# Sums of an attention sorted by DMA instead of transposed on TensorE

## The reference

```python
v = values.reshape(N, -1, HEADS, HEAD) @ Wv.T
k = keys.reshape(N, Lk, HEADS, HEAD) @ Wk.T
q = queries.reshape(N, Lq, HEADS, HEAD) @ Wq.T
energy = jnp.einsum('bqhd,bkhd->bhqk', q, k)
energy = jnp.where(mask, energy, jnp.float32(-1e+20))
attn = jax.nn.softmax(energy / np.sqrt(HEAD), axis=-1)
out = jnp.einsum('bhqk,bkhd->bqhd', attn, v).reshape(N, Lq, EMBED)
return out @ Wo.T + bo
...
x = x + jnp.tanh(g_xattn[1]) * _L1_xattn_ref(ctx_1024, ctx_1024, _layernorm(x, axis=-1), mask_1x1xSxS2_bk0, ...)
```

## Time and profile before

| | |
|---|---|
| median of 3 runs | 1335.78 us (1335.64 to 1337.21) |
| the profiled execution's own time | 1333.82 us |
| its span in the trace | 1332.1 us |
| second attention, first scores to last values product | about 231 to 382 us of the span |
| its projection and additions | about 386 to 413 us |
| busy in the whole span: PE, DVE, ACT, POOL | 1208.9, 1001.2, 835.0, 227.6 us |
| mean granted TensorE clock | 0.968 |

### The profile page before, as it was taken

How to read it: one execution, slowest core, us unless ns; L and a number is a source line. 1 busy time by engine, 2 the same in 40 slices (tenths; PEclk the granted TensorE clock), 3 DMA queues, 4 the chain that set the end, 5 groups by cost and what they waited for, 6 DMA issues and landing times.

```text
span 1332.1 us, 26357 instructions
## 1 busy us (share of the span) xinstructions
PE 1208.9 (91%) x10562; PEld 559.8 (42%) x10562; DVE 1001.2 (75%) x1491; ACT 835.0 (63%) x1484; POOL 227.6 (17%) x176
## 2 busy tenths in 40 slices
PE   4888964999999999778999999999999999999988
PEld 2566753555566456243333232323233333332237
DVE  4895695665536768458999999999999999999702
ACT  1224673777743642115888878787787878887861
POOL 2130124554742423800000000000000000000000
PEclk8979996999999999888999999999999999999999
DMA  6100027566500334812424533244423444243003
GB/s 189 26 1 15 1 31 166 96 110 129 96 1 1 119 119 144 124 24 49 64 51 76 86 60 65 53 87 80 57 59 67 87 64 67 50 82 50 2 1 126
DMA packets 78825, 92.55 MB, mean 69 GB/s; under 512 B 15210, under 2 KB 53356, under 8 KB 78704
## 3 DMA queue, kind: packets, MB, share of 16 engines
q1 hardware_dynamic: 78704, 90.87, 34.5%
HBM read 67.02 MB, written 23.80 MB: 68 GB/s over the span
## 4 chain that ended last, share of the span: by engine, by line
PE 60%; DVE 29%; ACT 5%; issue 2%; DMA 1%; SPq 1%; POOL 1%; DVEq 0%; ACTq 0%; POOLq 0%
DVE sm L2083 19%; PE ps L1554 10%; PE ps L1545 9%; PE ps L1526 6%; ACT W L1021 3%; PE ps L1415 3%; PE ps L1321 2%; PE ps L1664 2%; PE ps L1312 2%; PE ps L1313 2%; PE ps L1374 2%; PE ps L1481 1%; PE ps L1536 1%; PE ps L1279 1%; PE ps L1277 1%
## 5 line engine op out<-in xcount | busy, mean ns | idle before, releaser
L2083 DVE TENSOR_REDUCE sm<-ps 128x1 f32<-128x1024 f32 x512 | 599.7, 1218 | 31.4 <-PE ps L1526 28.1
L1021 ACT ACTIVATE W<-ps 128x512 f32<-128x512 f32 x1024 | 534.8, 605 | 139.2 <-PE ps L1554 135.2
L1554 PE MATMUL ps<-R 99*32 99x512 bf16 x4096 | 317.8, 383 | 6.2 <-ACT W L1021 3.2
L1545 PE MATMUL ps<-W,R 128*32 128x512 f32 x2048 | 265.6, 594 | 0.7 <-ACT W L1021 0.7
L1554 PEld LDWEIGHTS ps<-R 99*32 99x32 bf16 x4096 | 86.3, 94 | 224.4 <-ACT W L1021 168.0
L803 POOL COPY R<-R 128x512 f32<-128x512 f32 x16 | 9.8, 613 | 633.1 <-PE ps L1545 633.1
L1526 PE MATMUL ps<-R 50*128 50x512 bf16 x512 | 89.1, 388 | 15.8 <-DVE sm L2083 13.1
L1526 PE MATMUL ps<-KM,R 50*128 50x512 bf16 x512 | 87.3, 384 | 9.6 <-DVE sm L2083 6.6
L945 ACT ACTIVATE R<-ps 77x512 f32<-77x512 f32 x128 | 75.1, 592 | 23.6 <-PE ps L1313 14.2
L1545 PEld LDWEIGHTS ps<-W,R 128*32 128x32 f32 x2048 | 63.1, 111 | 42.1 <-ACT W L1021 1.4
L1866 DVE TENSOR_REDUCE small<-ps 128x4 bf16<-128x308 f32 x128 | 57.5, 473 | 23.5 <-PE ps L1279 23.4
(11 more groups left out here) (262 smaller groups left out, 1565.3 us busy)
## 6 DMA issues: line engine op xcount, KB each, us to landing
R<-x_parts SPq DMA_DIRECT2D x96, 128.0 KB, 4.9
R<-q_parts SPq DMA_DIRECT2D x192, 64.0 KB
R<-q_parts SPq DMA_DIRECT2D x96, 128.0 KB
R<-k_parts SPq DMA_DIRECT2D x96, 128.0 KB
x_parts<-R SPq DMA_DIRECT2D x8, 768.0 KB, 6.8
q_parts<-R SPq DMA_DIRECT2D x24, 256.0 KB, 2.6
k_parts<-R SPq DMA_DIRECT2D x24, 256.0 KB, 2.6
X<-in_x SPq DMA_DIRECT2D x4, 1024.0 KB, 9.8
```

The source lines that it names most:

```text
L1021: act.activation(PR[:, s % 2, h, :], third_bank("score", 64 * u + n), ACT.Exp, scale=0.25).then_inc(s_sfree, 1)
L1545: mm = pe.matmul(bank(7)[32 * h:32 * h + 32, :], VST[j][:, k, h, :], PR[:, s % 2, h, :], start=(k == 0), stop=(k == TB - 1))
L1554: mm = pe.matmul(o[32 * c:32 * c + 32, :], KST[j][0:MAX_ROW + 1, h, t:t + 32], QST[j][0:MAX_ROW + 1, h, 512 * (s // 8):512 * (s // 8) + 51 ...
L2083: dve.tensor_reduce(MX[:, half, h, q:q + 1], bank(2 * ((p + 1) % 2), 2), AX, ALU.max).then_inc(s_tfree, 1)
```

## The change

The sums stay with heads on partitions, as they come out of the values product. `out_transposes1`, `normalise1`, `transposes1` and ScalarE's copies of `OnT` go.

After `copy_out1(m)` SP issues eight DMAs, all inside SBUF (`sort_out1`): four take the denominator row of a head, 512 numbers in one partition, and spread it over 32 partitions of 16 numbers (`Rd1`, four half units deep), and four take the 16 rows of a head's sums to their place in `OT1`, which has the channels on the partitions and the tokens along the free axis, the form the projection reads. `copy_out1(m + 2)` waits for these DMAs of `m`, since it writes the same half of `Oe`.

VectorE inverts 128x16 denominators in place (`invert_sums1`, three half units behind). SP writes the inverses to DRAM (8 KB), waits until they have landed, and reads them back with each head's row given to 16 partitions (`spread_factors1`, three half units behind the sorting, 128 KB into `Den1`). Two units then lie on 128 partitions, and one multiplication of 128x512 divides both (`divide_pair1`). The projection of chunk `c` waits for the divisions of its batch alone; the last two divisions stand in VectorE's list behind the additions of the first batch and ahead of its statistics.

In SP's list the sorting and spreading of unit u - 3 stand behind `load_x_stack(u)` and the writes of parts. The semaphores of two bias steps are merged, which changes no wait.

```diff
+            def sort_out1(m):
+                u, q = m // 2, m % 2
+                b, rows, j = u // 4, 64 * (u % 2), u // 2 % 2
+                sp.wait_ge(s_oc, m + 1)
+                for h in range(4):
+                    sp.dma_start(Rd1[32 * h:32 * h + 32, m % 4, :],
+                                 Oe[32 * h + 16:32 * h + 17, q, :].rearrange("p (a n) -> p a n", a=32)
+                                 ).then_inc(s_od1[q], 16)
+                for h in range(4):
+                    v = slice(rows + 16 * h, rows + 16 * h + 16)
+                    sp.dma_start(OT1[v, j, b, 512 * q:512 * q + 512],
+                                 Oe[32 * h:32 * h + 16, q, :]).then_inc(s_od1[q], 16)
+
+            def spread_factors1(m):
+                u, q = m // 2, m % 2
+                pair, rows = u // 2, 64 * (u % 2)
+                sp.wait_ge(s_ri1, m + 1)
+                if u >= 1:
+                    sp.wait_ge(s_dd1[q], 32 * u)
+                sp.dma_start(DR1[m % 4].rearrange("(p n) -> p n", p=P), Rd1[:, m % 4, :]).then_inc(s_dd1[q], 16)
+                sp.wait_ge(s_dd1[q], 32 * u + 16)
+                if pair >= 2:
+                    sp.wait_ge(s_nd1, 2 * (pair - 2) + q + 1)
+                sp.dma_start(Den1[pair % 2][rows:rows + 64, q, :],
+                             DR1[m % 4].rearrange("(h n) -> h n", h=4).unsqueeze(1).to_broadcast([4, 16, 512])
+                             ).then_inc(s_dd1[q], 16)
+
+            def store_sums1(u):
+                for m in (2 * u, 2 * u + 1):
+                    sort_out1(m)
+                    if m >= 3:
+                        spread_factors1(m - 3)
...
             for u in range(UNITS):
...
                 load_x_stack(u)
                 for c in WRITES.get(u, ()):
                     write_parts(c)
+                if u >= 3:
+                    store_sums1(u - 3)
...
+            for u in range(UNITS - 3, UNITS):
+                store_sums1(u)
+            for m in range(2 * UNITS - 3, 2 * UNITS):
+                spread_factors1(m)
...
             def copy_out1(m):
                 act.wait_ge(s_pv, m + 1)
                 if m >= 2:
-                    act.wait_ge(s_ot1, m - 1)
+                    act.wait_ge(s_od1[m % 2], 128 * (m // 2))
                 act.copy(Oe[:, m % 2], bank(7)).then_inc(s_oc, 1)
...
-            for c in range(NC):
-                act.wait_ge(s_onT, c + 1)
-                if c >= 2:
-                    act.wait_ge(s_wo, c - 1)
-                act.copy(OnT[:, c % 2], bank(2 * (c % 2), 2).rearrange("p (j t) -> p j t", j=2)).then_inc(s_onc, 1)
...
-            def out_transposes1(m):
-                pe.wait_ge(s_oc, m + 1)
-                if m >= 1:
-                    pe.wait_ge(s_on, m)
-                for i in range(4):
-                    mm = pe.transpose(bank(3)[:, P * i:P * i + P], Oe[:, m % 2, P * i:P * i + P], identF[:, :])
-                mm.then_inc(s_ot1, 1)
...
-                if m >= 2:
-                    out_transposes1(m - 2)
...
-            pe.wait_ge(s_on, 2 * UNITS)
-            transposes1(0)
...
             for c in range(NC):
-                if c + 1 < NC:
-                    transposes1(c + 1)
-                pe.wait_ge(s_onc, c + 1)
+                b, q = c // 2, c % 2
+                pe.wait_ge(s_nd1, 4 * b + 3 + q)
                 if c == 1:
                     pe.wait_ge(s_qc, 3)
+                    pe.wait_ge(s_oc, 2 * UNITS)
...
-                        mm = pe.matmul(o, OnT[:, c % 2, j, P * i:P * i + P], wo1[:, j, :],
+                        mm = pe.matmul(o, OT1[:, j, b, 512 * q + P * i:512 * q + P * i + P], wo1[:, j, :],
...
-            def normalise1(m):
+            def invert_sums1(m):
+                dve.wait_ge(s_od1[m % 2], 128 * (m // 2 + 1))
+                if m >= 4:
+                    dve.wait_ge(s_dd1[m % 2], 32 * (m // 2 - 1))
+                dve.reciprocal(Rd1[:, m % 4, :], Rd1[:, m % 4, :]).then_inc(s_ri1, 1)
+
+            def divide_pair1(m):
                 u, q = m // 2, m % 2
-                b, hg = u // 4, u % 4
...
+                b, pair = u // 4, u // 2
+                dve.wait_ge(s_dd1[q], 32 * (u + 1))
+                o = OT1[:, pair % 2, b, 512 * q:512 * q + 512]
+                dve.tensor_tensor(o, o, Den1[pair % 2][:, q, :], ALU.mult).then_inc(s_nd1, 1)
...
-                if m >= 2:
-                    normalise1(m - 2)
+                if m >= 3:
+                    invert_sums1(m - 3)
+                if m >= 6 and (m - 6) // 2 % 2 == 1:
+                    divide_pair1(m - 6)
...
-            normalise1(2 * UNITS - 2)
-            normalise1(2 * UNITS - 1)
+            divide_pair1(2 * UNITS - 6)
+            invert_sums1(2 * UNITS - 3)
+            divide_pair1(2 * UNITS - 5)
+            invert_sums1(2 * UNITS - 2)
+            invert_sums1(2 * UNITS - 1)
...
             for b in range(B):
                 x3_batch(b)
+                if b == 0:
+                    divide_pair1(2 * UNITS - 2)
+                    divide_pair1(2 * UNITS - 1)
                 if b + 1 < B:
                     stats3(range(TB * b, TB * b + TB))
                     aggregate3(b)
```

More of the change, by code:

```diff
@@ L219, in build_program @@
               for v in (R4[0:SR1, 0:2048], R5[0:SR1, 0:2048], R5[0:SR1, 2048:4096])]
-        On = R1[:, :].rearrange("p (i c) -> p i c", i=NT)
-        OnT = R3f[:, 0:2048].rearrange("p (u j n) -> p u j n", u=2, j=2)
+        OT1 = R1[:, :].rearrange("p (j b t) -> p j b t", j=2, b=B)
+        Rd1 = R2f[:, 5946:6010].rearrange("p (u n) -> p u n", u=4)
+        Den1 = [v.rearrange("p (q n) -> p q n", q=2) for v in (R2f[:, 7168:8192], R3f[:, 7168:8192])]
         Mn = small[:, 464:496].bitcast(BF16).rearrange("p (u q j) -> p u q j", u=2, q=8)
-        rc1 = small[:, 528:544].rearrange("p (q j) -> p q j", q=4)
         s_w1 = sem("layer1_weights_loaded")
@@ L250, in build_program @@
         s_oc = sem("out1_copied")
[L251 to L255, removed]
+        s_od1 = [sem(f"out1_sorted{n}") for n in range(2)]
+        s_dd1 = [sem(f"out1_factors_moved{n}") for n in range(2)]
+        s_ri1 = sem("out1_recip")
+        s_nd1 = sem("out1_divided")
+        s_gb = sem("gated_biases")
+        s_xb = sem("biases_added")
         s_onT = sem("heads_transposed")
@@ L275, in score_bank1 @@
             return bank(4 + n % 3)
+        DR1 = nc.dram_tensor("sum_factors1", (4, 4 * 512), F32).ap()
         QP = nc.dram_tensor("q_parts", (3, B * C, S), BF16).ap()
@@ L351, in build_program @@
         s_c2 = sem("class_constants")
-        s_gb2 = sem("gated_bias2")
-        s_xb2 = sem("bias2_added")
         s_qp = sem("qkv_product")
@@ L781, in _ @@
             pool.tensor_tensor(qgn, qgn, mhalf[:, 0:2], ALU.pow).then_inc(s_qc, 1)
-            pool.tensor_scalar(bp2[:, :], bp2[:, :], gates[:, 3:4], None, ALU.mult).then_inc(s_gb2, 1)
+            pool.tensor_scalar(bp2[:, :], bp2[:, :], gates[:, 3:4], None, ALU.mult).then_inc(s_gb, 1)
             ln_rstd(3, range(B - 1))
@@ L812, in _ @@
                 pool.wait_ge(s_one, j + 1)
-            pool.wait_ge(s_gb2, 1)
+            pool.wait_ge(s_gb, 2)
             pool.wait_ge(s_xn, 4 * NC)
@@ L816, in _ @@
                 xs = X[:, TB * b:TB * b + TB, :]
-                pool.tensor_tensor(xs, xs, bp2[:, :].unsqueeze(1).to_broadcast([P, TB, C]), ALU.add).then_inc(s_xb2, 1)
+                pool.tensor_tensor(xs, xs, bp2[:, :].unsqueeze(1).to_broadcast([P, TB, C]), ALU.add).then_inc(s_xb, 1)
             for u in range(UNITS - 2):
@@ L1047, in _ @@
                 n = NC + c
-                act.wait_ge(s_onT, n + 1)
+                act.wait_ge(s_onT, c + 1)
                 if c >= 2:
@@ L1428, in _ @@
             transposes3(0)
-            pe.wait_ge(s_onc, NC)
             pe.wait_ge(s_wq3, 16)
@@ L1644, in transposes2 @@
                 if c >= 2:
-                    pe.wait_ge(s_onc, n - 1)
+                    pe.wait_ge(s_onc, c - 1)
                 for j in range(2):
@@ L1657, in _ @@
                     transposes2(c + 1)
-                pe.wait_ge(s_onc, n + 1)
+                pe.wait_ge(s_onc, c + 1)
                 if c >= 2:
@@ L1876, in maxima1 @@
                 reduce1(u, range(v.start + 2, v.stop))
-            def normalise1(m):
-                u, q = m // 2, m % 2
-                b, hg = u // 4, u % 4
[L1881 to L1889, removed]
+            def invert_sums1(m):
[4 more added lines that the diff above has]
+            def divide_pair1(m):
+                u, q = m // 2, m % 2
+                b, pair = u // 4, u // 2
+                dve.wait_ge(s_dd1[q], 32 * (u + 1))
+                o = OT1[:, pair % 2, b, 512 * q:512 * q + 512]
+                dve.tensor_tensor(o, o, Den1[pair % 2][:, q, :], ALU.mult).then_inc(s_nd1, 1)
             maxima1(0)
@@ L2139, in _ @@
                 dve.wait_ge(s_wo, NC + c + 1)
-                dve.wait_ge(s_xb2, c // 2 + 1)
+                dve.wait_ge(s_xb, B + c // 2 + 1)
```

## The result

The changed kernel takes 1495.55 us (median of 4 runs, 1490.64 to 1498.62) against 1335.71 us: a ratio of 1.119, 95% interval 1.1162 to 1.1218. It is slower by 160 us where 68 to 70 were forecast, and above the upper end of the range, 1470. The profiled execution took 1490.64 us with a span of 1488.9, 156.8 more than before.

What follows compares the result with a forecast made beforehand. SP's in-order issue queue was to bound the stage: loads 35.1, sorts 119.3, steps 66.1 and other issues 2.9 make 223.4 us; with the tail + 70.6 us on 1333.8, so 1404 us, range 1352 to 1470.

Steps and rivals of the forecast that it cites:

- What bounds the kernel after: Second attention: SP's in-order issue queue becomes the bound, 14.3 us a unit against TensorE's 8.2.
- the forecast names: Sign in the profile: ScalarE's copies, VectorE's reciprocals or TensorE's scores stand behind DMA.
- The price of a sorting issue: SP's queue, second attention: 0.466 us for each of 256 sorting DMAs, together 119.3 us.
- the dear end of my pitch: Upper bound for one sorting issue on SP, from a row spread into one partition: 0.608 us.
- the dear end of the whole sum: All SP prices at their upper bounds: 296 us of SP work, + 143 us, 1477 us.
- The wait after the write: SP waits 1.6 us for each write of inverses to land; with the read, 32 steps of 2.07 us.
- the fourth rival: Each unit's first inverses write lands late behind the six loads: 16 steps cost 3.3 us more, 1457 us; chance 0.07.
- The read back itself: SP's issue of each read back of the inverses, priced at 0.466 us.
- The tail: After SP's end at 461.3 us: last divisions, additions and projections end 21.3 us later, at 482.6; before, 411.99.
- the first rival: Second attention: sorts fit beside the rest, TensorE stays the bound, - 18.3 + 3.6 = - 14.7 us, 1319 us; chance 0.06.
- the third rival: Second attention: TensorE's clock falls to 0.50, its work 16.4 us a unit against SP's 14.3, 1451 us; chance 0.09.
- the mark of a TensorE near 60% busy: Sign that the forecast is right: TensorE near 60% busy in the second attention.

Runs made afterwards that it cites:

- e1: Changed kernel with the inverses read back one half unit after their write, denominators' buffer eight deep instead of four; 1442.12 us.
- e2: Changed kernel with four halves of Oe instead of two, so ScalarE's copy waits for the sorts of four half units before; 1495.28 us.
- e9: Changed kernel with eight more matmuls of 512 columns in each half unit, whose result nobody reads; 1494.59 us.
- b_forms: Kernel before the change with five bursts of DMAs of different forms added in an idle stretch of SP; 1331.03 us.
- e8: Changed kernel with the read back deferred one half unit, one denominators DMA instead of four, and ScalarE issuing the inverses' write and read back; 1409.37 us.
- e6: Changed kernel with the read back deferred one half unit, ScalarE issuing the sums DMAs, and eight unused matmuls more in each half unit; 1414.56 us.
- e11: As e8, with four matmuls of 512 columns more in each half unit, whose result nobody reads; 1385.99 us.
- e12_dram_warm: Changed kernel sorting through DRAM with five DMAs a half unit instead of ten, and two unused matmuls more in each; 1423.52 us.

## Why the prediction was wrong

*What bounds the kernel after: right.* SP issues from 238 to 546 us and waits only 0.7 us for another engine; the waits on ScalarE and VectorE have the forecast names; L1330 and L1355 are gone. e1, e2 and e9 leave SP's queue alone as the bound: 58 us of SP's waiting taken away gave 49 to 53, a deeper Oe and a better clock gave nothing.

*The price of a sorting issue: the first step that failed.* I took 0.466 us for a pitch, from loads of small rows over 16 partitions, as nearest in form. Those loads come from DRAM, and b_forms shows that such a load costs 0.420 to issue and a DMA of the same rows inside SBUF 0.589. Every row I had for this price has one end in DRAM; the likeness that counted was where the ends lie, not the rows or the bytes. Even the dear end of my pitch, 0.608, lies below the 0.634 measured. Summed over SP's timeline (start of an issue to the start of the next), the 256 sorts took 169.1 us where 119.3 were forecast: + 49.8. That is 0.661 each, since a few issues took up to 1.77 us. For this reason also the dear end of the whole sum, 1477, lies below the result.

*The wait after the write: the second.* 1.6 us was right for the second write of a unit, but not for the first, 2.8 to 4.8 us in ten of eleven units that have loads ahead of it, nor for the three at the end, 3.1 to 3.3. From write to read the 32 steps took 78.9 us where 32 x 1.6 = 51.2 were forecast: + 27.7, of which 22.5 in those ten and 4.6 in the three. This is the fourth rival, to which I gave 0.07; it came true beside the forecast, not in its place, and at about half of its price of 53. I made the forecast and it exclude each other, and so the range didn't hold their sum. The read back itself took 0.634 where 0.466 stood: 20.3 against 14.9, + 5.4. Loads and the rest add 2.0.

Together 84.9 us, and 0.2 for a later start: 85.1 on SP's end, 461.3 to 546.4.

*The tail: misread, and wrong both ways.* The prediction sets the end of the eighth projection after against 411.99, where only six have ended; six of 3.46 us with 0.87 between them already fill the time from 386.61. By its own terms the sixth would end 14.3 us behind SP, at 475.6, which is + 63.6 and not + 70.6. The slip of 7.0 us happened to bring the forecast nearer to the result; the first rival's 34 against 30.5 has it too. Measured, the sixth ends 18.5 us behind SP, 4.2 more: the last read lands 3.1 us behind SP's end instead of 1.6, and the fifth and sixth projection take 9.70 us instead of 6.9, at a clock of 0.50 until about 560 us after TensorE had waited 7.45. So 63.6 + 85.1 + 4.2 = 152.9 us at the sixth projection; the other 3.9 of the span come behind it and weren't followed up.

*The clock: the sign appeared, the price did not.* Granted 0.50 was there, as the third rival had it, and 16.4 us of TensorE work a unit with it, but SP's 19.3 are more, and a better clock gained nothing (e9). For the same reason the mark of a TensorE near 60% busy failed: at half speed its work filled 80 to 83% of the time. Late in e1 and e8, with SP relieved, the clock does set the pace.

*The first rival, faster,* is refuted: 20 issues in a unit beside six loads took SP far more than TensorE's 8.2 us. The Trainium skill (DMA: Bandwidth & Descriptors, Issuing engines are not separate DMA queues) calls the time to initiate a DMA usually small relative to the DMA itself. For these transfers the trace does not agree: 0.589 us of issue against 2.0 us to landing, and only the landings overlap. The Trainium skill (DMA: Bandwidth & Descriptors, Rules for kernel authors) tells to join many small transfers, since below 64 KB one pays mostly for overhead. The trace agrees, with 0.589 us for 32 KB and for 1 KB alike.

## What to carry to other kernels

Count the DMA issues that a change puts on one queue, price them by issues of the same form (where both ends lie, and how the rows are cut), and set the sum against the period of the loop: here 20 more issues a unit outweighed 0.59 us saved twice on the bounding engine. If the trace has no such issue, a burst of them in an idle stretch of the kernel before gives the price, as b_forms did. A queue that waits for its own write may stand longer when a large transfer was issued shortly ahead (2.8 to 4.8 us here, not 1.6); read back one step later. When several rivals can hold at once, add their prices into the range. Count the projections, or whatever the tail consists of, on both sides before comparing their ends.

## What the runs showed of the hardware

In bursts of like DMAs into an idle queue an issue took SP 0.589 us with both ends in SBUF and 0.420 with one end in DRAM, for the same 16 rows; 1 KB cost as much as 32 KB. Other forms with an end in DRAM took more, 0.520 and 0.579 for the inverses' write and read back.

TensorE's granted clock fell to 0.50 (1.2 GHz) after TensorE had waited for the queues: in the changed kernel first between 258 and 262 us, where it was busy 1.46 of 4 us. It could stay there though TensorE was busy all the time: 16 of 16 us in e8, 49.77 of 50 in e1, and in e8 from 282 to 320 us, 38 of 38, after which it rose without a wait of TensorE in between. The kernel before keeps 1.00 at 150.66 of 151. Matmuls without use, put where TensorE would have waited, held it at 0.91 to 1.00 in e6 (eight in a half unit) and e11 (four), and at 0.75 to 0.88 in e9 (eight); with two, in e12_dram_warm, it fell to 0.50.
